# Packed counts and two-part hop tables, with sixteen batches of destinations done densely, in a graph kernel of three passes

## The chip, the cores and the metric

The kernel runs on one NeuronCore of a Trainium2 chip. The metric is the device time of one execution, in microseconds. Five engines matter: PE multiplies matrices, DVE and ACT do elementwise work, POOL issues the gathers of rows, and SP issues nearly all other transfers. Each engine runs its own list of instructions in order, and semaphores tie the lists together.

## What is computed

12,500 nodes with 128 features each, and 212,500 edges sorted by destination (self loops included). Two graph layers follow each other, each behind a layer norm, a ReLU and with a residual:

```python
def reference(x, src, dst, edge_type_2, W_data, b_data, W_control, b_control, W_self, b_self):
    h = relu(layernorm(x))
    # layer 0: a typed message for each edge, summed by destination
    msg = where(edge_type == 0, h[src] @ W_data.T + b_data, h[src] @ W_control.T + b_control)
    x = x + relu(segment_sum(msg, dst) + h @ W_self.T + b_self)
    # layer 1: two hops with symmetric degree norm
    h = relu(layernorm(x)); y = out = h
    for _ in range(2):
        y = segment_sum(y[src] * norm[:, None], dst)
        out = out + y
    return x + out / 3
```

(Names are shortened; `norm` is the product of the inverse square roots of both ends' degrees.)

## The kernel before

The nodes lie in 98 blocks of 128, four blocks to a batch (25 batches, the last with two blocks). The edges lie in 208 groups of 1024, eight chunks of 128 to a group; the last group has five chunks.

After a preparation (messages for each node and type to `typed_table`, indices, bases of the groups) three passes run, k = 0, 1, 2. Each is a loop over slots, and each engine has the same loop with its own part of a slot.

A group, in any pass: POOL issues one indirect DMA for each chunk (`gather`, L874), which brings 128 rows of 512 bytes from the pass's table into a place of `rows` (a ring of `RING` = 4 groups). DVE makes masks that tell to which node of a 128-node window each edge goes (`make_hot`, L1465, in `hot`, a ring of 3, made two groups ahead). PE multiplies mask by rows, eight fp32 matmuls (`sum_rows`, L1091). DVE adds the result to `sums` (`add_group`, L1487). When a batch has all its groups, `cut` closes it, and three slots later `finish` turns it into the next pass's rows: DVE scales (L1395 to L1404), SP stores `scaled` to `hop_table` (`store_nodes`, L732) and the rest to `resid`.

Pass 0 walks all 208 groups. The destinations of the first 15 batches (`DENSE_BATCHES`) are also prepared for the hops: a count of edges from each source node to each destination of a tile of 128 (60 tiles). DVE makes four cells at a time (`make_quad`, a quad; L1509 and L1512 compare cell numbers with `count_up` in PSUM), PE multiplies them (`make_cells`, L1135), ACT turns the 98 x 4 counts of a cell into bytes (`keep_cell`, L1002), and SP stores each tile's strip in DRAM. Between these PE runs matmuls that nothing reads (`fill`, L1126), sixteen per slot in all. The first hop's operand stays in SBUF: `table_parts` holds each scaled block as a high part, rounded to fp32r, and the rest (ACT L982, DVE L1413).

The hops (k = 1, 2) do the first 15 batches by dense products and only the rest by gathering: 82 groups each. A dense step is 14 blocks of one tile's strip against their blocks of `table_parts`: SP loads 224 KB of byte counts (`load_counts`, L772, a ring of `COUNT_RING` = 7 steps; the load for step n + 7 waits until step n is cast), ACT casts them to fp32r (`cast_counts`, L1011, a ring of 3), PE runs 14 matmuls of 256 columns (`dense_step`, L1175). A tile has 7 steps, a hop 420. 18 (hop 1) and 15 (hop 2) of them are lead steps, run behind the last group of the pass before; the others are spread over `DENSE_SLOTS` = 80 of the 82 slots. In hop 1 the last four tiles are done piece by piece, so that pieces of `table_parts` come free early. `read_tile` (L1542) takes a finished tile into `own_in`, and `finish` treats it as a batch.

For hop 2 `table_parts` must hold hop 1's result. SP reloads it from `hop_table` in 14 pieces of 448 KB (`reload`, L783) into a ring of three; ACT copies the high part (`part_high`, L1016), DVE subtracts (`part_low`). These stand in ACT's and DVE's lists ahead of the slot's finish and casts.

What sets the order: in a slot PE sums its group, then runs the slot's dense steps. ACT does reload copies, then the finish, then the slot's casts. DVE adds the group before, makes masks, reads tiles of the slot before, then reload parts and the finish. SP loads counts behind ACT's casts, then reloads, then stores the batch finished one slot before, then loads nodes for a coming one. POOL waits before group o until group o - `RING` is summed, and at the start of a hop until the whole table is stored.

A branch for unevenly spread edges exists on all engines; it isn't taken here.

## Time and profile before

| | us |
|---|---|
| median of 3 runs | 3999.4 (3997.6 to 4004.5) |
| the profiled execution's span | 3997.9 |
| PE busy | 3405.9 (85%) |
| POOL busy | 2879.8 (72%) |
| ACT busy | 2329.7 (58%) |
| DVE busy | 2186.3 (55%) |
| first dense lead step of hop 1 | at 2240.7 |
| slot 0 of hop 1, slot 0 of hop 2 | at 2277.0, at 3158.1 |
| last dense step of hop 2 ends | at 3987.1 |

Busy time is what the profiler saw an engine execute; POOL's issue gaps between gathers aren't in it. The chain of work that ended last goes 38% through POOL's gathers and 34% through the dense matmuls. The three passes have different limits, so a share of the whole span says little; the rows below are from single stretches. A matmul's own duration is longer than its distance to the next, since matmuls overlap; distances between starts are what counts.

### The profile page before, as it was taken

The page shows a single profiled execution, that of the slowest core. Times are in us where ns is not written, and L with a number is a line of the kernel's source. Part 1 is how long each engine was busy: PE and PEld are TensorE (multiplying, and loading weights), DVE is VectorE, ACT ScalarE, POOL GpSimd, SP SyncE. Part 2 cuts the span into 40 slices and gives each one's busy share as a digit, 9 for nine tenths or more (in the row PEclk, how much of TensorE's full clock was granted, in tenths as well). Part 3 has the DMA queues.
Part 4 walks back from the last instruction along what each step waited for, and adds up shares of the span by engine and source line. Part 5 has one row for each costly group of instructions (what it writes and reads, how often), then busy time and mean ns, then how long its engine had stood idle before and what let it go on. Part 6 is the DMA issues. An engine that isn't in the chain of part 4 may idle for free.

```text
span 3997.9 us, 62254 instructions
## 1 busy us (share of the span) xinstructions
PE 3405.9 (85%) x23420; PEld 2729.2 (68%) x23420; DVE 2186.3 (55%) x3333; ACT 2329.7 (58%) x3075; POOL 2879.8 (72%) x3058
## 2 busy tenths in 40 slices
PE   7666777777777787777777899999998899999999
PEld 4344444444444444444444799999998899999999
DVE  7523888888888888888888422222222222222222
ACT  4001444444444444444444688888887788888887
POOL 2677777777777777777777577777776477777775
PEclk9788998999999999999999999999999999999999
DMA  6222333333333334333333566666666666666665
GB/s 194 85 61 61 109 119 121 113 109 110 126 109 110 114 110 128 110 109 125 110 115 112 170 179 187 192 192 187 189 189 184 179 179 176 187 182 181 179 184 145
DMA packets 367268, 571.77 MB, mean 143 GB/s; under 512 B 66678, under 2 KB 308225, under 8 KB 359283
## 3 DMA queue, kind: packets, MB, share of 16 engines
q1 hardware_dynamic: 270435, 370.74, 29.6%
q0 software_dynamic: 95664, 196.60, 19.2%
q8 instruction: 188, 3.08, 0.3%
q14 instruction: 117, 0.96, 0.1%
q10 hardware_dynamic: 864, 0.39, 0.0%
HBM read 424.48 MB, written 142.99 MB: 142 GB/s over the span
## 4 chain that ended last, share of the span: by engine, by line
PE 44%; POOL 38%; issue 13%; DVE 2%; DMA 2%; ACT 1%; SPq 0%; DVEq 0%; POOLq 0%; ACTq 0%
POOL rows L874 38%; PE wide L1175 34%; PE sums_bank L1091 7%; PE wide L1056 1%; ACT strip_ring L1011 1%; DMA stage<-hop_table 1%; DMA rows<-typed_table,index 0%; PE turned_bank L1126 0%; DVE big L1214 0%; DVE rows L1254 0%; DVE stage L1512 0%; POOL stage L914 0%; PE wide L1135 0%; DMA stage<-strips 0%; DMA big<-in_x 0%
## 5 line engine op out<-in xcount | busy, mean ns | idle before, releaser
L874 POOL DMA_INDIRECT rows<-typed_table,index x1661 | 1589.0, 957 | 506.0 <-issue 505.0
L874 POOL DMA_INDIRECT rows<-hop_table,index x1306 | 1251.9, 959 | 481.4 <-issue 394.9
L1011 ACT CAST strip_ring<-stage 128x1792 fp32r<-128x1792 uint8 x840 | 1409.2, 1687 | 285.3 <-PE wide L1175 279.2
L1175 PE MATMUL wide<-table_parts,strip_ring 128*128 128x256 f32 x11760 | 1461.0, 285 | 35.7 <-ACT strip_ring L1011 35.7
L1175 PEld LDWEIGHTS wide<-table_parts,strip_ring 128*128 128x128 f32 x11760 | 1431.3, 193 | 38.0 <-ACT strip_ring L1011 17.5
L1002 ACT CAST stage<-wide 128x392 uint8<-128x392 f32 x1920 | 790.3, 502 | 983.9 <-PE wide L1135 982.6
L1126 PE MATMUL turned_bank<-all_twos 128*128 128x512 bf16 x3328 | 1112.0, 394 | 0.0
L1091 PE MATMUL sums_bank<-rows,hot 128*128 128x129 f32 (+1 forms) x5934 | 801.2, 292 | 287.0 <-DMA rows<-typed_table,index 272.6
L1091 PEld LDWEIGHTS sums_bank<-rows,hot 128*128 128x128 f32 x5934 | 764.4, 206 | 337.8 <-issue 304.0
L1512 DVE TENSOR_TENSOR stage<-count_up,stage 128x1568 bf16<-128x1568 f32 x480 | 855.4, 1782 | 0.0
L1135 PE MATMUL wide<-stage 128*128 128x392 bf16 x1920 | 652.6, 340 | 221.8 <-DVE stage L1512 220.0
L1487 DVE SCALAR_TENSOR_TENSOR sums<-sums_bank,in_upper,sums 128x129 f32 (+1 forms) x372 | 129.8, 349 | 1064.8 <-PE sums_bank L1091 1042.6
L1126 PEld LDWEIGHTS turned_bank<-all_twos 128*128 128x128 bf16 x3328 | 339.0, 102 | 344.6 <-issue 53.5
L1135 PEld LDWEIGHTS wide<-stage 128*128 128x128 bf16 x1920 | 191.9, 100 | 460.2 <-DVE stage L1512 317.5
L1465 DVE TENSOR_TENSOR hot<-count_up,local 128x1024 f32<-128x1024 f32 x372 | 451.8, 1215 | 0.1
L1509 DVE TENSOR_TENSOR stage<-count_up,stage 128x512 bf16<-128x512 f32 x480 | 328.2, 684 | 174.2 <-PE wide L1135 174.0
L1542 DVE TENSOR_REDUCE own_in<-wide 128x128 f32<-128x256 f32 x120 | 50.8, 423 | 356.9 <-PE wide L1175 356.9
L976 ACT ACTIVATE batch_spread<-batch_spread 128x8 f32<-128x8 f32 x25 | 5.4, 216 | 249.6 <-DVE batch_spread L1225 249.6
L1487 DVE SCALAR_TENSOR_TENSOR sums<-sums_bank,base_all,sums 128x129 f32 (+1 forms) x372 | 127.8, 343 | 0.4
L1056 PE MATMUL wide<-stage,rows 128*128 128x384 f32 x196 | 78.5, 528 | 0.0
L1413 DVE TENSOR_TENSOR table_parts<-stage,table_parts 128x896 fp32r<-128x896 f32 x14 | 15.3, 1092 | 73.6 <-ACT table_parts L1016 73.6
L1402 DVE SCALAR_TENSOR_TENSOR xin<-scaled,xin 128x512 f32<-128x512 f32 (+1 forms) x50 | 34.2, 684 | 37.9 <-ACT scaled L945 35.1
(141 smaller groups left out, 669.5 us busy)
## 6 DMA issues: line engine op xcount, KB each, us to landing
stage<-strips SPq DMA_DIRECT2D x840, 224.0 KB
strips<-stage SPq DMA_DIRECT2D x60, 1568.0 KB
rows<-typed_table,index POOLq DMA_INDIRECT x1661
rows<-hop_table,index POOLq DMA_INDIRECT x1306
resid<-xin SPq DMA_DIRECT2D x50, 256.0 KB, 3.0
hop_table<-scaled SPq DMA_DIRECT2D x50, 256.0 KB, 3.8
xin<-resid SPq DMA_DIRECT2D x50, 256.0 KB
typed_table<-rows SPq DMA_DIRECT2D x49, 256.0 KB, 2.1
```

What stands on the lines that cost most here:

```text
L874: pool.indirect_dma_start(out=rows[:, o % RING, c, 0:P], out_offset=None, in_=tables[k], in_offset=bass.IndirectOffsetOnAxis(ap=index[:, c ...
L1002: act.copy(count_strips[tile % 2][:, :, w * CELL:(w + 1) * CELL], wide[:, nth % CELL_BANKS, 0:real_blocks * CELL].rearrange("p (b n) -> p ...
L1011: act.copy(strip_ring[:, number % STRIP_RING], counts_ring[place]).then_inc(strip_cast, 1)
L1056: last = pe.matmul(wide[:, i % 2 * PAIR + b, 0:KINDS * P], normed_t[i % 2][:, b * P:(b + 1) * P], w_all[:, :], start=True, stop=True)
L1091: last = pe.matmul(sums_bank[:, bank, 0:columns], hots[:, c, :], rows[:, slot, c, 0:columns], start=(c == 0), stop=(c == size - 1))
L1126: pe.matmul(turned[:, 0:4 * P].rearrange("p (n f) -> p n f", n=4), all_twos[:, :], all_twos[:, :].unsqueeze(1).to_broadcast([P, 4, P]), st ...
L1135: pe.matmul(wide[:, nth % CELL_BANKS, 0:real_blocks * CELL], quad_low[quad % 2][:, w, :], quad_hot[quad % 2][:, w, :], start=True, stop=Tr ...
L1175: last = pe.matmul(wide[:, nth % 4, 0:PARTS * P], strip_ring[:, number % STRIP_RING, b - first, :], table_parts[:, b, :, :].rearrange("p n ...
L1465: dve.tensor_tensor(hot[:, place, :, :], counting(CHUNKS, P), local[:, group * CHUNKS:(group + 1) * CHUNKS].unsqueeze(2).to_broadcast([P, ...
L1487: last = dve.scalar_tensor_tensor(out=into, in0=sums_bank[:, o % 2, 0:columns], scalar=inside_tile, in1=into, op0=ALU.mult, op1=ALU.add)
L1509: dve.tensor_tensor(quad_low[place], counting(QUAD, P), cell_low[:, cells].unsqueeze(2).to_broadcast([P, QUAD, P]), ALU.is_equal)
L1512: dve.tensor_tensor(quad_hot[place], counting(QUAD, columns), cell_key[:, cells].unsqueeze(2).to_broadcast([P, QUAD, columns]), ALU.is_equ ...
```

## The change

- Hop tables (`hop_table`) hold high part and rest side by side, 1 KB per node where it was 512 bytes. `finish` makes both parts for hop 1's batches too, in `new_parts`, and SP stores them from there, behind `low_ready`.
- Group sums of the hops take fp32r masks and rows of 256 columns; DVE adds both halves, four operations in place of two.
- A reload goes straight into `table_parts`, 896 KB a piece, without work on ACT or DVE; PE waits for its pieces.
- Counts of pass 0: two cells share one matmul result width (2 x 196 columns), since a value carries the count of an even node and, with weight 256, that of the odd one beside it. ACT turns two cells at once into 16-bit words (`keep_pair`). The wide compare has 784 elements in place of 1568, on 16-bit numbers; the narrow compare is four operations with a weight each.
- Sixteen batches are dense: 64 tiles, 448 steps per hop, 73 groups per hop. `DENSE_SLOTS` is 69.
- The rings are smaller: rows 3 groups, masks 2 (made one group ahead), counts 6 steps; three groups are gathered early in place of four.

```diff
-RING = 4
-HOT_RING = 3
-EARLY = 4
+RING = 3
+HOT_RING = 2
+EARLY = 3
...
+CELL_PAIRS = CELLS // 2
+COUNT_BASE = 256
...
-DENSE_BATCHES = 15
+DENSE_BATCHES = 16
...
-COUNT_RING = 7
+COUNT_RING = 6
...
-RELOAD_RING = 3
 RELOADS_AT_ONCE = 3
-STAGE_WORDS = 11264
-DENSE_SLOTS = 80
+STAGE_WORDS = 10112
+DENSE_SLOTS = 69
...
-    tables = [typed_table] + [nc.dram_tensor(f"hop_table{n}", (padded, P), F32, kind="Internal").ap() for n in range(HOPS)]
+    tables = [typed_table] + [nc.dram_tensor(f"hop_table{n}", (real_blocks * P, PARTS * P), F32, kind="Internal").ap() for n in range(HOPS)]
...
+        rows = sbuf("rows", [RING, CHUNKS, PARTS * P], F32R)
+        hot = sbuf("hot", [HOT_RING, CHUNKS, P], F32R)
 
...
-        reloaded = [region(reload_words) for _ in range(RELOAD_RING)]
+        new_parts = [region(NODE_BLOCKS * PARTS * P, F32R).rearrange("p (b n f) -> p b n f", b=NODE_BLOCKS, n=PARTS)
+                     for _ in range(2)]
 
...
+        def parts_of(n, k, s, general):
+            if general or k:
+                return new_parts[n % 2][:, 0:held(s)]
+            return table_parts[:, s * NODE_BLOCKS:s * NODE_BLOCKS + held(s)]
 
...
-            def store_nodes(n, k, s):
+            def store_nodes(n, k, s, general):
                 if k < HOPS:
                     sp.wait_ge(resid_ready, n + 1)
                     sp.dma_start(of_batch(resid, s), in_blocks(xin[:, n % XIN, :])).then_inc(resid_stored[n % XIN], 16)
-                    sp.wait_ge(scaled_ready, n + 1)
-                    sp.dma_start(of_batch(tables[k + 1], s), in_blocks(scaled[:, n % 2, :])).then_inc(table_stored[n % 2], 16)
+                    sp.wait_ge(low_ready, n + 1)
+                    first, end = s * BATCH, s * BATCH + held(s) * P
+                    sp.dma_start(tables[k + 1][first:end, :].rearrange("(b p) f -> p b f", p=P),
+                                 parts_of(n, k, s, general).rearrange("p b n f -> p b (n f)").bitcast(F32)
+                                 ).then_inc(table_stored[n % 2], 16)
                     return
                 first, end = s * NODE_BLOCKS, min((s + 1) * NODE_BLOCKS, whole)
...
-                def reload(r, piece):
+                def reload(piece):
                     for s in reload_batches(piece):
                         n = event_of[1][s]
                         sp.wait_ge(table_stored[n % 2], 16 * count_of(n + 1, 2, n % 2))
                     sp.wait_ge(strip_used, last_step_with(piece) + 1)
-                    if r >= RELOAD_RING:
-                        sp.wait_ge(reload_low, r - RELOAD_RING + 1)
                     first = piece * RELOAD_BLOCKS
-                    sp.dma_start(in_blocks(reloaded[r % RELOAD_RING], RELOAD_BLOCKS),
+                    sp.dma_start(table_parts[:, first:first + RELOAD_BLOCKS].rearrange("p b n f -> p b (n f)").bitcast(F32),
                                  tables[2][first * P:(first + RELOAD_BLOCKS) * P, :].rearrange("(b p) f -> p b f", p=P)
-                                 ).then_inc(reload_in[r % RELOAD_RING], 16)
+                                 ).then_inc(reload_in[piece], 16)
...
                     pool.indirect_dma_start(
-                        out=rows[:, o % RING, c, 0:P], out_offset=None, in_=tables[k],
+                        out=rows[:, o % RING, c, 0:width_of(k)].bitcast(F32), out_offset=None, in_=tables[k],
...
-            def finish(n, k, s, splits):
+            def finish(n, k, s, general):
...
-                if splits:
-                    first, blocks = s * NODE_BLOCKS, held(s)
+                if k < HOPS:
                     act.wait_ge(scaled_ready, n + 1)
-                    act.copy(table_parts[:, first:first + blocks, 0, :], in_blocks(scaled[:, n % 2, 0:blocks * P], blocks)).then_inc(high_ready, 1)
+                    act.copy(parts_of(n, k, s, general)[:, :, 0, :], in_blocks(scaled[:, n % 2, 0:held(s) * P], held(s))
+                             ).then_inc(high_ready, 1)
...
-                def part_high(r, piece):
-                    first = piece * RELOAD_BLOCKS
-                    act.wait_ge(reload_in[r % RELOAD_RING], 16 * (r // RELOAD_RING + 1))
-                    act.copy(table_parts[:, first:first + RELOAD_BLOCKS, 0, :], in_blocks(reloaded[r % RELOAD_RING], RELOAD_BLOCKS)
-                             ).then_inc(reload_high, 1)
-
...
-                                    keep_cell(quad * QUAD + w)
-                        if k == 1:
-                            for r, piece in reloads_of_slot(i - 1):
-                                part_high(r, piece)
+                                for w in range(QUAD // 2):
+                                    keep_pair(quad * QUAD // 2 + w)
                         finishing = event_at(k, i - 3)
-                        if finishing and k == 0:
-                            finish(finishing[0], k, finishing[1], True)
+                        if finishing and k < HOPS:
+                            finish(finishing[0], k, finishing[1], False)
...
-            def sum_rows(bank, slot, size, hots, columns):
+            def sum_rows(k, bank, slot, size, hots):
                 for c in range(size):
-                    last = pe.matmul(sums_bank[:, bank, 0:columns], hots[:, c, :], rows[:, slot, c, 0:columns],
-                                     start=(c == 0), stop=(c == size - 1))
+                    ends = dict(start=(c == 0), stop=(c == size - 1))
+                    if k == 0:
+                        last = pe.matmul(sums_bank[:, bank, 0:TILE], hots[:, c, :].bitcast(F32), rows[:, slot, c, 0:TILE].bitcast(F32), **ends)
+                    else:
+                        last = pe.matmul(sums_bank[:, bank, 0:PARTS * P], hots[:, c, :], rows[:, slot, c, :], **ends)
                 return last
...
                     elif tile < LEAD_TILES:
-                        pe.wait_ge(reload_low, reloads_before(first, end))
+                        for piece_in in range(first // RELOAD_BLOCKS, (end - 1) // RELOAD_BLOCKS + 1):
+                            pe.wait_ge(reload_in[piece_in], 16)
...
                                          op0=ALU.mult, op1=ALU.add).then_inc(resid_ready, 1)
                 dve.tensor_tensor(in_blocks(values, blocks), in_blocks(values, blocks), over_features(factors, blocks), ALU.mult
                                   ).then_inc(scaled_ready, 1)
-                if splits:
-                    dve.wait_ge(scaled_ready, n + 1)
-                    part_low(s * NODE_BLOCKS, blocks, in_blocks(values, blocks), high_ready, n + 1, low_ready)
-
-            def part_low(first, blocks, values, parted, count, ready):
-
-                dve.wait_ge(parted, count)
-                dve.tensor_tensor(table_parts[:, first:first + blocks, 1, :], values,
-                                  table_parts[:, first:first + blocks, 0, :].bitcast(F32), ALU.subtract).then_inc(ready, 1)
+                dve.wait_ge(scaled_ready, n + 1)
+                dve.wait_ge(high_ready, n + 1)
+                parts = parts_of(n, k, s, general)
+                dve.tensor_tensor(parts[:, :, 1, :], in_blocks(values, blocks), parts[:, :, 0, :].bitcast(F32), ALU.subtract
+                                  ).then_inc(low_ready, 1)
...
-                        last = dve.scalar_tensor_tensor(out=into, in0=sums_bank[:, o % 2, 0:columns], scalar=inside_tile, in1=into,
-                                                        op0=ALU.mult, op1=ALU.add)
-                    last.then_inc(added, 1)
+
+                    def add_columns(start):
+                        for n, inside_tile in enumerate((in_upper[:, group:group + 1], in_lower[:, group:group + 1])):
+                            into = flat_sums[:, ds(base - tile_place(first) + n * TILE, columns)]
+                            last = dve.scalar_tensor_tensor(out=into, in0=sums_bank[:, o % 2, start:start + columns], scalar=inside_tile,
+                                                            in1=into, op0=ALU.mult, op1=ALU.add)
+                        return last
+
+                    if k:
+                        add_columns(0).then_inc(half_added, 1)
+                        dve.wait_ge(half_added, o - groups + 1)
+                        add_columns(P).then_inc(added, 1)
+                    else:
+                        add_columns(0).then_inc(added, 1)
...
-                    columns = real_blocks * CELL
-                    dve.tensor_tensor(quad_hot[place], counting(QUAD, columns),
-                                      cell_key[:, cells].unsqueeze(2).to_broadcast([P, QUAD, columns]), ALU.is_equal
+                        dve.wait_ge(strip_made, (quad - 1) * QUAD // 2)
+                    first = quad * QUAD % (CELL_BATCHES * P)
+                    for w in range(QUAD):
+                        cell = slice(first + w, first + w + 1)
+                        dve.tensor_scalar(quad_low[place][:, w, :], count_up, cell_low[:, cell], cell_weight[:, cell],
+                                          ALU.is_equal, ALU.mult)
+                    dve.tensor_tensor(quad_hot[place], count_quads,
+                                      cell_key[:, first:first + QUAD].unsqueeze(1).to_broadcast([P, hot_columns, QUAD]), ALU.is_equal
                                       ).then_inc(strip_hot_ready, 1)
...
-                        if i < slots_of(k) and o + 2 < n_places:
-                            make_hot(o + 2)
+                        if i < slots_of(k) and o + 1 < n_places:
+                            make_hot(o + 1)
...
-                        if k == 1:
-                            for r, piece in reloads_of_slot(i - 1):
-                                part_low(piece * RELOAD_BLOCKS, RELOAD_BLOCKS, in_blocks(reloaded[r % RELOAD_RING], RELOAD_BLOCKS),
-                                         reload_high, r + 1, reload_low)
```

## Rows read from the trace of the kernel before

**Rows 1.** Stretches: us, busy PE, PEld, DVE, ACT, POOL (instructions), PE clock, DMA share, GB/s

```profile
1000.00:1100.00 100.00, 76.86 (x435) 45.29 (x434) 85.36 (x114) 46.95 (x114) 75.92 (x80) 0.93 0.40 126
...
2500.00:2600.00 100.00, 100.00 (x848) 100.00 (x847) 26.29 (x49) 82.30 (x50) 75.66 (x80) 1.00 0.68 190
```

**Rows 2.** Page, group of POOL's gathers in pass 1: count, busy, mean ns, idle before

```profile
L874 POOL DMA_INDIRECT rows<-typed_table,index x1661 | 1589.0, 957 | 506.0 <-issue 505.0
```

**Rows 3.** PE in order of time: start, us, instructions; then page, dense matmuls

```profile
2277.01 1.95 PE L1091 MATMUL sums_bank<-rows,hot 128*128 128x128 f32 x16
...
2288.87 1.95 PE L1091 MATMUL sums_bank<-rows,hot 128*128 128x128 f32 x16
...
2299.04 1.94 PE L1091 MATMUL sums_bank<-rows,hot 128*128 128x128 f32 x16
...
L1175 PE MATMUL wide<-table_parts,strip_ring 128*128 128x256 f32 x11760 | 1461.0, 285 | 35.7 <-ACT strip_ring L1011 35.7
```

**Rows 4.** POOL and PE in order of time: a gather, then the sum of its group

```profile
129.06 1.65 POOL L874 DMA_INDIRECT rows<-typed_table,index  x1 [0.30 <-issue]
...
143.04 3.81 PE L1091 MATMUL sums_bank<-rows,hot 128*128 128x129 f32 x16 [14.12 <-DVE hot L1465]
...
1910.35 0.94 POOL L874 DMA_INDIRECT rows<-typed_table,index  x1 [0.30 <-issue]
...
1925.32 1.95 PE L1091 MATMUL sums_bank<-rows,hot 128*128 128x129 f32 x16
...
2254.71 0.94 POOL L874 DMA_INDIRECT rows<-hop_table,index  x1 [23.06 <-DMA hop_table<-scaled]
```

**Rows 5.** PE in order of time, end of hop 1 and start of hop 2

```profile
3061.28 11.13 PE L1175 MATMUL wide<-table_parts,strip_ring 128*128 128x256 f32 x70 [5.79 <-ACT strip_ring L1011]
...
3117.66 3.06 PE L1091 MATMUL sums_bank<-rows,hot 128*128 128x128 f32 x26
...
3158.06 1.95 PE L1091 MATMUL sums_bank<-rows,hot 128*128 128x128 f32 x16
```

**Rows 6.** Groups of instructions by line and form: ACT's copies of reloaded tables

```profile
L1016 ACT CAST table_parts<-stage 128x896 fp32r<-128x896 f32 x14 | 13.1, 937 | 35.7 <-DMA stage<-hop_table 35.7
```

**Rows 7.** PE in order of time, the last sums of hop 2

```profile
3987.10 3.06 PE L1091 MATMUL sums_bank<-rows,hot 128*128 128x128 f32 x26
```

**Rows 8.** Groups by line and form, DVE and ACT: busy us, mean ns of one

```profile
L1011 ACT CAST strip_ring<-stage 128x1792 fp32r<-128x1792 uint8 x840 | 1409.2, 1687 | 285.3 <-PE wide L1175 279.2 <-DMA stage<-strips 6.1
...
L1512 DVE TENSOR_TENSOR stage<-count_up,stage 128x1568 bf16<-128x1568 f32 x480 | 855.4, 1782 | 0.0
...
L1509 DVE TENSOR_TENSOR stage<-count_up,stage 128x512 bf16<-128x512 f32 x480 | 328.2, 684 | 174.2 <-PE wide L1135 174.0
...
L1542 DVE TENSOR_REDUCE own_in<-wide 128x128 f32<-128x256 f32 x120 | 50.8, 423 | 356.9 <-PE wide L1175 356.9
...
L1413 DVE TENSOR_TENSOR table_parts<-stage,table_parts 128x896 fp32r<-128x896 f32 x14 | 15.3, 1092 | 73.6 <-ACT table_parts L1016 73.6
...
L982 ACT CAST table_parts<-scaled 128x512 fp32r<-128x512 f32 x24 | 14.8, 617 | 32.7 <-DVE scaled L1404 32.7
...
L1395 DVE TENSOR_TENSOR scaled<-own_in,inv 128x512 f32<-128x512 f32 x15 | 10.2, 679 | 0.0
...
L1530 DVE SCALAR_TENSOR_TENSOR stage<-wide,cell_line 128x128 f32<-128x128 f32 x15 | 4.2, 283 | 2.8 <-PE wide L1153 2.8
```

**Rows 9.** DMA queues in 2500 to 2600, then 250 to 350: packets, MB, share

```profile
q1 hardware_dynamic: 11808, 13.60, 46.1%
q0 software_dynamic: 2553, 5.22, 20.9%
...
stage<-strips SPq DMA_DIRECT2D x49, 224.0 KB
...
q1 hardware_dynamic: 3168, 1.57, 5.5%
```

**Rows 10.** GB/s of all transfers in 2.5 us slices from 1000 us

```profile
GB/s 347 321 135 52 59 52 52 52 52 52 133 401 266 52 52 56 52 52 52 214 127 52 59 52 52 52 52 267 321 288 85 54 52 52 52 52 114 396 284 67
```

More of the change, by code:

```diff
@@ L608, in reloads_of_slot @@
         def reloads_of_slot(i):
-            return [(r, piece) for r, (slot, piece) in enumerate(reload_order) if slot == i]
-        def reloads_before(first, end):
-            return max(r for r, (_, piece) in enumerate(reload_order)
-                       if piece * RELOAD_BLOCKS < end and (piece + 1) * RELOAD_BLOCKS > first) + 1
+            return [piece for slot, piece in reload_order if slot == i]
         assert all(lead_steps[k] <= LEAD_AT_ONCE * LAST for k in range(1, HOPS + 1))
@@ L1353, in take_degrees, with finish @@
                 dve.tensor_scalar(spread_now[:, 1, :], degree, 1.0, None, ALU.max).then_inc(degree_read, 1)
-            def finish(n, k, s, source, read, splits, own=None):
+            def finish(n, k, s, source, read, general, own=None):
                 blocks = held(s)
```

115 lines of the change are left out of this document (67 added, 48 removed).

## The prediction

> **What bounds the kernel now.** I read the stretches first, then for each stretch the engine that never pauses, then the seams between stretches.
>
> Pass 1 runs to about 2235 us. In a 100 us stretch of it POOL is busy 75.9 us, and the rest is the 0.30 us gap behind each of its 80 gathers [rows 1, 2]: one gather costs 1.25 us, a group of eight 10.0 us, and in 1661 gathers POOL waits 1 us in all for anything but its own issuing [rows 2]. PE (77 us of 100) and DVE (85) have room. Pass 1 is POOL's.
>
> In the hops PE is busy 100 us of 100, and POOL still issues 80 gathers per 100 us [rows 1]. A slot is one group summed and five dense steps: 2288.87 to 2299.04, 10.17 us. Slot 0 has six steps and lasts 11.86 us [rows 3], so a step (14 matmuls of 256 columns) costs 1.69 us, 0.121 us a matmul, and the eight fp32 matmuls of a group 1.72 us. POOL begins hop 1 at 2254.71 [rows 4], 22 us ahead of slot 0, and keeps that lead. So PE sets the hops, with POOL 2% behind it: cheaper matmuls alone would soon meet POOL, and only fewer gathers let both fall.
>
> The ideal length of hop 1's dense slots is 402 x 1.69 + 80 x 1.72 = 817 us (420 steps less 18 lead steps). The rows show 2277.01 to 3117.66, 840.7 us [rows 3, 5]: 24 us are stalls, all at the end, where PE waits for strips, as 5.79 us at 3061.28 [rows 5]. ACT is late because its list there holds copies of reloaded tables: it waits 35.7 us for their transfers [rows 6] and casts nothing meanwhile. From 3117.66 to slot 0 of hop 2 at 3158.06 are 40.4 us [rows 5]; from there to 3987.10, 829 us; from there to the end 10.8 [rows 7].
>
> **The change, part by part.** *Pass 1.* The sixteenth batch adds one gather of cells, 1.25 us on POOL: +1.3 us. The count work (512 quads for 480) isn't on POOL. A quad costs DVE 1.78 + 0.68 us now [rows 8]. Its new wide compare has 784 elements, half of 1568: 0.9 us if it goes by elements, up to the 1.09 us of the 896-element subtraction; the four low compares are 0.15 us each (128 of 512 elements) to 0.28 (the 128-element op from PSUM) [rows 8]. That is 1.5 to 2.2 us a quad, 4.2 to 6.2 us per slot against 6.5 now, so the cover stays and I take nothing. If DVE exceeded 10 us a slot, the excess would count in full.
>
> The ring of rows falls from four groups to three. The latest sum of pass 1 began 15 us after POOL issued its group's last gather (1910.35 to 1925.32, largest of 207 pairs) [rows 4]; with its 1.95 us that is 17, and POOL needs the place 20 us after that issue began. So no wait. At the start the first sum comes 14 us after its group and takes 3.8 us: 18 against 20.
>
> *Gathers.* Hop groups fall from 82 to 73, each gather brings 1 KB rows, and sums become 256-column fp32r matmuls. That is the dense form, so I take 0.121 us, 0.97 us a group. The dearest it could be is today's 1.72 us. POOL's cost goes by rows, 128 as before: 10.0 us a group against a slot that becomes longer, so POOL drops off the path.
>
> *Dense work.* 448 steps a hop, 430 in slots in hop 1 and 433 in hop 2 (18 and 15 lead steps), over 69 slots: 430 x 1.69 + 69 x 0.97 = 793.6 us and 433 x 1.69 + 67 = 798.7 us. A slot is 11.5 us. ACT casts 1.68 us a step [rows 8], 10.5 us a slot: it keeps only 1 us of slack where it had 1.8.
>
> *ACT's new place in hop 1.* The split of a finished batch into high and rest parts moves from the reload to the finish. So ACT waits, once per batch, for DVE's scaled values, copies them in 0.62 us, and the next slot's casts are queued behind. DVE in turn first reads tiles of the slot before. From a tile's last matmul: read 0.42, three steps of the finish near 0.7 each with their waits, 2.5 us; then copy 0.62 and cast 1.68 [rows 8]. PE meanwhile has the d steps behind that tile and one group sum. The stall is 2.6 + 0.62 + 1.68 + 0.3 - 0.97 - 1.69 d, or 4.2 - 1.7 d. The planner's formulas give d = 1 for two batches, d = 2 for eight, and three or more (or no tile) for the rest: 2 x 2.5 + 8 x 0.9 = 12 us. Between the ends 0 (ACT ahead through other slack) and 24 x 4.2 = 101 I take 12.
>
> *Transfers.* In the hop stretch the row queue takes 20.9% of 16 engines for 80 gathers, 4.2 us a gather. The other queue takes 46.1% for 49 strips and nine batch transfers; these cost 14.7 us each (six in 5.5%), so a strip costs 12.4 [rows 9]. After: strips 6.2 x 12.4 = 77, batch traffic 20, gathers 8 x 4.2 to 8 x 8.4 (by row, or by byte) = 34 to 67. That is 131 to 164 us of 184 per slot, 71 to 89%; now it is 68%. I take the upper part of it. Strips are asked for six steps ahead, now seven. A batch's three transfers then hold the queue 3.5 us; I put 3 us of stalls on hop 2.
>
> *Reloads.* ACT's and DVE's splits go, and with them the 24 us. But each piece is now 896 KB, near 50 us of engine time, and eight of them are asked for between slots 64 and 68, on the same queue as the strips. In these 45 us: 24 strips 300, gathers 270, reloads 400, others 50, together 1020 us against 720. That is 19 us too much; prefetched strips and rows absorb a part. I take 12 us, with 0 and 20 as ends. The Trainium skill's page "DMA: Bandwidth & Descriptors", section Specifications, gives one core near 358 GB/s of HBM. By that the 18 MB of this stretch need 51 us, 6 more than it has. The trace has slices of 396 and 401 GB/s [rows 10], above that limit, though those are stores of counts.
>
> *Seam.* Slots 69 to 72 hold sums alone. With three places POOL can't issue group 72 before group 69 is summed, so its five gathers (6.3 us) and the landing put that sum 10 us past the dense end, where it was done after 3. Now ACT casts no lead strip before batch 23 is split: DVE adds (four operations a group now), makes masks and finishes batches 15 and 23, which brings ACT to about 15 us; the first lead step starts near 17, and 15 lead steps take 25.4. The seam is 42.4 us. Batch 24 is stored by then (25 us) and POOL's first group landed (37 us). Late reloads have the 25 us too. At the end of hop 2: sum at 10, adds, clearing, finish, store: 16.5 us where it is 10.8.
>
> **Sum.** 2277.0 + 1.3 = 2278.3. Hop 1: 793.6 + 12 + 12 = 817.6 -> 3095.9. Seam 42.4 -> 3138.3. Hop 2: 798.7 + 3 -> 3940.0. End 16.5 -> 3956.5, against a span of 3997.9: 41 us less. The median lies 1.5 us above the span, so 3958. Of the 41 us, 23 come from each hop's ideal, 19 from stalls replaced by smaller ones; the ends give 8 back.
>
> **Rivals.** *Nothing collides (3931).* The 12, 12 and 3 us don't appear. For it: in the whole trace PE waits for strips only 35.7 us, all near seams [rows 3]. Against: ACT's slack halves. 0.18.
>
> *Transfers pace the hops (3986).* Late strips cost 0.2 us per slot, 138 slots, 28 us. For it: 89% is an average, and batch traffic comes in bursts. Against: today's strips are never late inside a hop. To lose the whole gain a slot must reach 11.8 us, which needs 189 us of transfers, or 11.5 us a gather against at most 8.4. 0.17.
>
> *ACT is held at each finish (slower, up to 4046).* If DVE answers so late that each of 24 finishes costs the full 4.2 us, 88 us come on top. It decides at 2.2 us each: 12 + 41 = 53 over 24. For it: ACT, DVE and PE then wait in a ring. Against: DVE is busy 26 us of 100 in the hops [rows 1]. 0.07.
>
> *The change doesn't do what it says (4068).* If fp32r masks and rows cost what fp32 costs now, each of 146 groups is 0.75 us dearer, +110 us. Against: the dense rows have the very form. 0.04.
>
> *A port lock in pass 1.* DVE's new count operations read and write 16-bit values; were each of the 2048 small compares to hold POOL's descriptor writes for its 0.15 us, pass 1 would grow by 300 us. For it nothing: in the midst of pass 1 POOL's gathers keep 0.94 us [rows 4]. The Trainium skill's page "SBUF — State Buffer", section Who interferes with whom, has VectorE lock GpSimd out in its two-port modes; the counting operand stays in PSUM here, which the skill excludes from them. 0.02.
>
> **Chances.** Forecast 0.52; 3931: 0.18; 3986: 0.17, of which 0.05 lie within no change; the three slower ones 0.13, of which 0.01 does, as a mild form. A measurement of this kernel tells 0.2% (8 us) from no change. Faster 0.82, same 0.06, slower 0.12. The range takes in 3931, below it 10 us for the seam and masks, and 3986, above it the rest of the transfer bounds: 3920 to 4000.
>
> **What would show it.** Hop slots of 11.5 us with PE full; group sums at 0.97 us; POOL waiting for PE in each hop slot; pass 1 unchanged and gathers at 1.25 us; in hop 1 short PE waits for strips behind finishes, none in hop 2; the last sum some 10 us behind the last dense step; no copies of reloaded tables on ACT. Wrong would be: transfers near 100%, slots above 11.8 us, a gather above 1.3 us, or POOL waiting for sums in pass 1.

## The result

| | median, us | lowest to highest | ratio to before (95% interval) |
|---|---|---|---|
| before | 3998.5 | 3997.6 to 4004.5 | |
| after | 3954.5 | 3953.1 to 3955.9 | 0.9889 (0.9877 to 0.9901) |
| after, once more, beside the experiments | 3951.1 | 3948.8 to 3957.6 | 0.9887 (0.9870 to 0.9903) |

The change takes 44 us off: 3954.5, where 3958 was forecast. The profiled execution of the kernel after has a span of 3952.7 us (3956.5 was summed). In its time line the places of the sum can be read one by one (us):

| | before | forecast | after |
|---|---|---|---|
| slot 0 of hop 1 begins | 2277.0 | 2278.3 | 2281.6 |
| dense slots of hop 1 last | 840.7 | 817.6 | 810.0 |
| from there to slot 0 of hop 2 | 40.4 | 42.4 | 49.7 |
| dense slots of hop 2 last | 829.0 | 801.7 | 794.2 |
| from there to the end | 10.8 | 16.5 | 17.2 |

Stretches of the kernel after, one in pass 1 and one in hop 1 (columns as in [rows 1]):

```profile
1000.00:1100.00 100.00, 80.97 (x427) 49.91 (x425) 65.91 (x199) 29.55 (x62) 75.62 (x81) 0.90 0.36 111
2500.00:2600.00 100.00, 99.01 (x825) 98.60 (x824) 29.50 (x60) 90.93 (x58) 65.97 (x69) 1.00 0.81 243
```

In pass 1 POOL's 75.6 us are what they were [rows 1], though DVE fell from 85 to 66 us and ACT from 47 to 30. In the hop PE is still full, POOL fell from 75.7 to 66.0 us and now has slack, ACT rose to 91 and the transfers from 68% to 81%.

Groups of the page after, in the columns of [rows 2] and [rows 3] (the gathers of pass 1, ACT's casts, the dense matmuls, the gathers of the hops, the group sums of the hops):

```profile
L890 POOL DMA_INDIRECT rows<-typed_table,index x1661 | 1589.9, 957 | 506.1 <-issue 505.9
L1027 ACT CAST strip_ring<-stage 128x1792 fp32r<-128x1792 uint8 x896 | 1494.4, 1688 | 137.8 <-PE wide L1188 115.5
L1188 PE MATMUL wide<-table_parts,strip_ring 128*128 128x256 f32 x12544 | 1539.0, 284 | 28.6 <-ACT strip_ring L1027 26.0
...
L890 POOL DMA_INDIRECT rows<-hop_table,index x1162 | 1109.7, 955 | 599.7 <-issue 314.2
...
L1102 PE MATMUL sums_bank<-rows,hot 128*128 128x256 f32 x1162 | 163.6, 284 | 15.8 <-DMA rows<-hop_table,index 10.6
```

A gather of 1 KB rows costs POOL 955 ns, one of 512 byte rows 957: its cost goes by rows, as taken. Beyond that, POOL waits in the hops 240 us for group sums, where it waited 3 us for them before:

```profile
POOL rows L890 <- PE sums_bank L1102: 239.9, 135, 7.4
```

(From the waits of POOL between 2280 and 3950: us in all, times, longest.) PE in order of time shows an undisturbed slot, group sum and six steps:

```profile
2294.23 1.11 PE L1102 MATMUL sums_bank<-rows,hot 128*128 128x256 f32 x8
2295.18 10.22 PE L1188 MATMUL wide<-table_parts,strip_ring 128*128 128x256 f32 x84
2305.24 1.11 PE L1102 MATMUL sums_bank<-rows,hot 128*128 128x256 f32 x8
```

From start to start the sum takes 0.95 us, the six steps 10.06, the slot 11.01. A slot of seven steps takes 12.68. Of 69 slots 16 have seven: 16 x 12.68 + 53 x 11.01 = 786.4 us is the ideal of hop 1, and 23.6 of its 810.0 us are stalls.

### The profile page after: what moved, and what is told of

Its sections match the earlier page's. It is cut to its first block, busy times and chain, and to the rows that moved or that the text cites. A ratio compares the mean times of both kernels' runs of the same rounds, so it can differ in the third digit from the quotient of the medians.

```text
span 3952.7 us, 62194 instructions
## 1 busy us (share of the span) xinstructions
PE 3401.3 (86%) x22892; PEld 2748.3 (70%) x22892; DVE 1925.3 (49%) x5238; ACT 2121.5 (54%) x2246; POOL 2739.2 (69%) x2915
## 4 chain that ended last, share of the span: by engine, by line
PE 41%; POOL 40%; issue 13%; DVE 2%; DMA 2%; ACT 1%; SPq 0%; POOLq 0%; DVEq 0%; ACTq 0%
POOL rows L890 40%; PE wide L1188 36%; PE sums_bank L1102 3%; ACT strip_ring L1027 1%; PE wide L1063 1%; DMA stage<-strips 1%; POOL stage L930 0%; DVE big L1232 0%; DVE flat L1272 0%; DMA hop_table<-stage 0%; DVE xin L1420 0%; DVE scaled L1413 0%; DMA big<-in_x 0%; DVE scaled L1422 0%; PE turned_bank L1136 0%
## 5 line engine op out<-in xcount | busy, mean ns | idle before, releaser
L1188 PEld LDWEIGHTS wide<-table_parts,strip_ring 128*128 128x128 f32 x12544 | 1524.5, 193 | 32.2 <-ACT strip_ring L1027 17.1
L890 POOL DMA_INDIRECT rows<-hop_table,index x1162 | 1109.7, 955 | 599.7 <-issue 314.2
L1018 ACT CAST stage<-wide 128x392 uint16<-128x392 f32 x1024 | 497.0, 485 | 1277.9 <-PE wide L1145 1271.6
L1100 PE MATMUL sums_bank<-rows,hot 128*128 128x129 f32 x3322 | 514.9, 319 | 362.5 <-DMA rows<-typed_table,index 346.1
L1538 DVE TENSOR_SCALAR stage<-counts,stage 128x128 bf16<-128x128 int16 x2048 | 559.6, 335 | 470.2 <-PE wide L1145 469.9
L1145 PE MATMUL wide<-stage 128*128 128x196 bf16 x2048 | 687.5, 336 | 99.1 <-DVE stage L1540 99.1
L1507 DVE SCALAR_TENSOR_TENSOR sums<-sums_bank,in_upper,sums 128x128 f32 (+1 forms) x500 | 174.7, 349 | 915.4 <-PE sums_bank L1102 676.3
L1483 DVE TENSOR_TENSOR hot<-counts,local 128x1024 fp32r<-128x1024 int16 x354 | 429.5, 1213 | 0.1
L1540 DVE TENSOR_TENSOR stage<-counts,stage 128x784 bf16<-128x784 int16 x512 | 283.7, 554 | 0.0
L1102 PE MATMUL sums_bank<-rows,hot 128*128 128x256 f32 x1162 | 163.6, 284 | 15.8 <-DMA rows<-hop_table,index 10.6
L1507 DVE SCALAR_TENSOR_TENSOR sums<-sums_bank,base_all,sums 128x128 f32 (+1 forms) x500 | 171.2, 342 | 0.7
```

The lines of the kernel that those rows point to most:

```text
L890: pool.indirect_dma_start(out=rows[:, o % RING, c, 0:width_of(k)].bitcast(F32), out_offset=None, in_=tables[k], in_offset=bass.IndirectOff ...
L1018: act.copy(paired_strips[tile % 2][:, :, w * CELL:(w + 1) * CELL].rearrange("p b (c n) -> p b c n", c=2), wide[:, nth % CELL_BANKS, 0:2 * ...
L1100: last = pe.matmul(sums_bank[:, bank, 0:TILE], hots[:, c, :].bitcast(F32), rows[:, slot, c, 0:TILE].bitcast(F32), **ends)
L1102: last = pe.matmul(sums_bank[:, bank, 0:PARTS * P], hots[:, c, :], rows[:, slot, c, :], **ends)
L1145: made = pe.matmul(wide[:, nth % CELL_BANKS, half * hot_columns:(half + 1) * hot_columns], quad_low[quad % 2][:, w, :], quad_hot[quad % 2] ...
L1188: last = pe.matmul(wide[:, nth % 4, 0:PARTS * P], strip_ring[:, number % STRIP_RING, b - first, :], table_parts[:, b, :, :].rearrange("p n ...
```

## The experiments

The kernel after ran again in the first set, to tell its own spread from the rest:

> The changed kernel again, as the reference of this set: 3954 us.

Ratios are to the kernel before, run on the same chip beside them (its median is 3998.9 beside a1 and e1 to e3, 4000.1 beside e4 to e9).

| kernel | median, us | ratio (95% interval) |
|---|---|---|
| e1: before, sixteen batches in 69 slots | 4064.1 | 1.0160 (1.0143 to 1.0177) |
| e2: after, fifteen batches in 78 slots | 3942.3 | 0.9862 (0.9846 to 0.9879) |
| e3: before, counts packed | 4000.8 | 1.0006 (0.9997 to 1.0016) |
| e4: after, three casts ahead of the finish | 3941.4 | 0.9854 (0.9838 to 0.9870) |
| e5: after, half of each reload | 3940.3 | 0.9848 (0.9832 to 0.9865) |
| e7: e4 with 71 slots | 3934.6 | 0.9837 (0.9820 to 0.9853) |
| e9: e2 with e4's order | 3938.1 | 0.9845 (0.9828 to 0.9861) |

### e1. The sixteenth batch alone

```
-DENSE_BATCHES = 15
+DENSE_BATCHES = 16
...
-DENSE_SLOTS = 80
+DENSE_SLOTS = 69
```

> The kernel before with sixteen dense batches, dense steps over 69 slots, and nothing else of the change (fp32 sums, 512-byte rows, unpacked counts). Theory (PE sets the hops): a slot is 6.2 steps of 1.68 us and a sum of 1.79 us, 12.2 us; the dense slots of a hop take 843 and 848 us where they ideally take 817 and 822, the reload stalls of 24 us and the seams stay, pass 1 gets 1.3 us longer. Together about 4055 us, 55 slower than before. Rival (fewer gathers are what saves): 72 gathers less in each hop at 1.25 us, 90 us a hop, about 3820 us. A second rival: DVE's 512 unpacked quads (2.46 us each, 90% of a slot in pass 1) begin to delay sums, and pass 1 ends more than 5 us later as well.

It costs 65 us. PE in order of time, at the end of hop 1:

```profile
3061.94 11.99 PE L1175 MATMUL wide<-table_parts,strip_ring 128*128 128x256 f32 x98
...
3082.23 12.17 PE L1175 MATMUL wide<-table_parts,strip_ring 128*128 128x256 f32 x84 [6.51 <-ACT strip_ring L1011]
...
3118.88 12.57 PE L1175 MATMUL wide<-table_parts,strip_ring 128*128 128x256 f32 x84 [5.12 <-ACT strip_ring L1011]
```

An added batch is 28 steps, 47 us of PE in each hop, for nine groups dropped, 16 us of PE with fp32 sums. PE set the hops already, so the time rises: the dense slots of the two hops last 28 and 27 us longer (869.0 and 855.9), the seam 7 and the end 3, with four sums behind the last dense slot and not two. Pass 1 isn't later (slot 0 of hop 1 at 2276.4), though DVE was busy 90 us of 100 in it.

### e2. All the rest without it

```
-DENSE_BATCHES = 16
+DENSE_BATCHES = 15
...
-DENSE_SLOTS = 69
+DENSE_SLOTS = 78
```

> The changed kernel with fifteen dense batches again (82 groups a hop, dense steps over 78 slots); two-part tables, fp32r sums, direct reloads and packed counts stay. Theory: a slot needs 9.6 us of PE and 10.0 us of POOL, so POOL sets the hops: 653 gathers take 816 us from POOL's start near 2256 to 3074, about 18 us from the last sum to its restart, 816 us again and some 12 us to the end: about 3920 us, and PE waits for rows in most slots. Rival (the sixteenth batch carries the gain): about 3998 us, as before. Third: 1 KB rows at POOL's full pace need 89% of the transfer engines; if they can't keep up, slots pass 10.4 us and the time 3950 us.

It is faster than the kernel after, by 9 to 12 us. The stretch 2500 to 2600 and, in order of time, PE and then POOL:

```profile
2500.00:2600.00 100.00, 100.00 (x838) 100.00 (x838) 36.06 (x73) 91.15 (x59) 75.93 (x80) 1.00 0.84 258
```

```profile
2505.34 1.11 PE L1102 MATMUL sums_bank<-rows,hot 128*128 128x256 f32 x8
2506.29 8.54 PE L1188 MATMUL wide<-table_parts,strip_ring 128*128 128x256 f32 x70
2514.66 1.11 PE L1102 MATMUL sums_bank<-rows,hot 128*128 128x256 f32 x8
...
3083.05 2.04 PE L1102 MATMUL sums_bank<-rows,hot 128*128 128x256 f32 x8 [8.59 <-DMA rows<-hop_table,index]
3090.01 1.41 PE L1102 MATMUL sums_bank<-rows,hot 128*128 128x256 f32 x5 [4.91 <-DMA rows<-hop_table,index]
```

```profile
3083.87 0.95 POOL L890 DMA_INDIRECT rows<-hop_table,index  x1 [0.30 <-issue]
3105.10 0.94 POOL L890 DMA_INDIRECT rows<-hop_table,index  x1 [20.28 <-DMA hop_table<-stage]
```

A five-step slot needs 9.32 us of PE against 10.0 of POOL. POOL now runs from 2256.7 to 3083.9 with 0.9 us of waits for sums, and the last sums wait for its rows. So POOL sets the length of the hops, as the theory said. But PE doesn't wait for rows in most slots, though that was expected: in the stretch shown PE is full, since it had lost time to ACT in three slots (as behind 2492.1, 13.24 us) and works that off; from 2707 on it catches up with POOL again and again. It waits for rows 30 times in the two hops, 56 us in all, 35 of them behind the last dense slots. The price of a hop is what POOL costs: 82 groups in 828 us and 20.3 us until the next table is stored, 848 in all from POOL's start in hop 1 to its start in hop 2. The kernel after needs 810.0 + 49.7 = 859.7 from slot 0 to slot 0. The expected 3920 was too low by 19 us. Nearly all of it is the gathers: 653 of them were put at 816 us a hop and took 828 and 824, since some last 1.1 to 1.5 us and not 0.95. From slot 0 of hop 1 (2281.4) to slot 0 of hop 2 (3123.8) e2 takes 842.4 us, 17.3 less than the kernel after, and from there to the end (3938.8) 815.0, 3.6 more. How the gain over the kernel before divides between fp32r sums and direct reloads was not tried.

### e3. The packed counts alone

The wide compare and the low compares, ACT's copy of pairs and PE's pairs, put into the kernel before:

```
...
-                    dve.tensor_tensor(quad_low[place], counting(QUAD, P), ...)
...
+                    for w in range(QUAD):
...
+                        dve.tensor_scalar(quad_low[place][:, w, :], count_up, cell_low[:, cell], cell_weight[:, cell], ...)
...
```

> The kernel before with the packed counts alone (two cells in one result, 784-element compare, half of ACT's copies); all else as before. Theory: pass 1 is set by POOL's gathers, and the count work lies beside them: the end of pass 1 within 1 us, the time within 3 us of 3998. Rival (the count work is on the path of pass 1): DVE falls by 10 to 20 points of the stretch, and pass 1 is shorter by tens of us. Third: 16-bit operations of DVE lock POOL out, gathers above 1.25 us and pass 1 longer.

No change: the interval reaches from 0.9997 to 1.0016. The stretch 1000 to 2200 of the kernel before and of this one:

```profile
1000.00:2200.00 1200.00, 920.92 (x5105) 551.24 (x5105) 1017.39 (x1355) 548.04 (x1332) 909.26 (x955) 0.92 0.37 115
```

```profile
1000.00:2200.00 1200.00, 952.38 (x5109) 601.63 (x5110) 777.47 (x2317) 337.64 (x708) 909.29 (x955) 0.89 0.37 115
```

240 us of DVE and 210 of ACT are gone from this stretch, and POOL's busy time is the same to 0.03 us. Work was taken from engines that had cover. Slot 0 of hop 1 begins at 2273.8, 3.2 us earlier than before, where 1 us was expected at most; but the kernel after differs by 5 us from run to run in this place (2281.6 and 2276.2), and the medians show no gain.

### e4. ACT's finish behind three casts

```
+                        now = steps_at(k, i)
+                        ahead = min(3, len(now)) if k == 1 and i <= 64 else 0
+                        for number in now[:ahead]:
+                            cast_counts(number)
                         ...finish...
-                        for number in steps_at(k, i):
+                        for number in now[ahead:]:
                             cast_counts(number)
```

> The changed kernel, but in the dense slots of hop 1 up to slot 64 ACT does the first three casts of a slot ahead of the finish's copy, and only then waits for DVE's scaled values. Theory (ACT's wait inside its list makes the ten short PE waits of hop 1, 10.9 us in slot lengths): all ten vanish, every slot of hop 1 up to 64 is 11.01 or 12.68 us, and the time falls by 11 us, to about 3942. Rival (the strips come late because transfers are at 81%): the waits stay where they are, since the order on ACT moves no transfer, time 3953. Third: DVE, now held longer by ACT at each finish, delays masks or adds, and new waits on DVE appear in PE's sums: slower.

Ten slots of the kernel after are longer than 11.01 or 12.68 us before slot 64, one of them this (ACT, then PE, in order of time):

```profile
2446.48 0.62 ACT L997 CAST stage<-scaled 128x512 fp32r<-128x512 f32 x1 [3.28 <-DVE scaled L1422]
```

```profile
2445.50 1.11 PE L1102 MATMUL sums_bank<-rows,hot 128*128 128x256 f32 x8
2448.74 11.84 PE L1188 MATMUL wide<-table_parts,strip_ring 128*128 128x256 f32 x84 [2.13 <-ACT strip_ring L1027]
2460.42 1.11 PE L1102 MATMUL sums_bank<-rows,hot 128*128 128x256 f32 x8
```

With the casts first, the same stretch of this kernel's PE:

```profile
2448.09 1.11 PE L1106 MATMUL sums_bank<-rows,hot 128*128 128x256 f32 x8
2449.05 10.22 PE L1192 MATMUL wide<-table_parts,strip_ring 128*128 128x256 f32 x84
2459.10 1.11 PE L1106 MATMUL sums_bank<-rows,hot 128*128 128x256 f32 x8
```

All ten are gone: every slot to 3029.59 takes 11.01 or 12.69 us, and the dense slots of hop 1 last 797.2 us in place of 810.0. So the waits were ACT's order, and nothing else took their place. The slots of the reloads are as long as before (11.9, 16.4 and 15.6 us).

### e5. Half of each reload

The rest parts keep their old values, so hop 2 computes with them; all the rest is done.

```
-  sp.dma_start(table_parts[:, first:first + RELOAD_BLOCKS].rearrange(...).bitcast(F32),
-               tables[2][first * P:(first + RELOAD_BLOCKS) * P, :]...
+  sp.dma_start(table_parts[:, first:first + RELOAD_BLOCKS, 0, :].bitcast(F32),
+               tables[2][first * P:(first + RELOAD_BLOCKS) * P, 0:P]...
```

> The changed kernel with each reload cut to the high parts (448 KB for 896); the rest parts in table_parts keep hop 1's old values, so hop 2's dense products are computed from wrong rest parts. Theory (the reloads on the strips' queue delay the strips at the end of hop 1): the stalls of slots 64 to 68 (11 us) fall to 4 us or less, and the 2.7 us wait for a strip inside the lead steps shrinks as well; together 8 to 11 us less, about 3944. Rival (SP's wait for the last use of a piece, which holds back the next strip loads, is the cause, not the bytes): the stalls stay above 8 us and the time within 3 us of 3953.

PE in order of time, first of the kernel after, then of this one:

```profile
3047.23 1.11 PE L1102 MATMUL sums_bank<-rows,hot 128*128 128x256 f32 x8
...
3064.03 12.97 PE L1188 MATMUL wide<-table_parts,strip_ring 128*128 128x256 f32 x84 [3.18 <-ACT strip_ring L1027]
...
3091.54 2.07 PE L1102 MATMUL sums_bank<-rows,hot 128*128 128x256 f32 x16
```

```profile
3057.99 1.11 PE L1102 MATMUL sums_bank<-rows,hot 128*128 128x256 f32 x8
3058.94 10.22 PE L1188 MATMUL wide<-table_parts,strip_ring 128*128 128x256 f32 x84
3068.99 1.11 PE L1102 MATMUL sums_bank<-rows,hot 128*128 128x256 f32 x8
```

The three reload slots of the kernel after take 12.5, 17.1 and 14.7 us; here they take 11.01, 11.00 and 11.45. The order of SP's list and the number of transfers are the same, so the cause is the bytes. The 2.7 us wait inside the lead steps was expected to shrink with them and did not (2.78 us at 3112.13): it has another cause, shown below where the seam is explained. The queues of the kernel after from 3045 to 3092 (packets, MB, share of 16 engines) show the load:

```profile
DMA packets 12675, 16.31 MB, mean 347 GB/s; under 512 B 1012, under 2 KB 11735, under 8 KB 12673
...
q1 hardware_dynamic: 11255, 12.43, 80.5%
q0 software_dynamic: 1418, 3.84, 23.7%
```

The shares add to 104%, so the packets of this stretch took more engine time than it has, and ACT waits up to 4.4 us for its strips.

### e7. e4 with 71 slots

```
-DENSE_SLOTS = 69
+DENSE_SLOTS = 71
```

> The kernel of casts first (above), with the dense steps over 71 slots in place of 69. Theory (behind the last dense step the last group's sum waits 12 us since its rows can't be asked for before group 69 is summed): with two dense slots more the rows are there, the last sum ends 3 us behind the last dense step; the two slots add 2 us a hop, the end of hop 2 shrinks from 17 us to about 11, net 4 to 5 us less there and 0 to 5 less at the seam: 3932 to 3938. Rival (the finish of the last batches, not the sum, ends the hop): the end stays at 17 us and the time at that of casts first or 2 to 4 us above.

This asks what the sums cost that stand alone behind the dense slots. PE at both ends of a hop:

```profile
3076.70 1.71 PE L1106 MATMUL sums_bank<-rows,hot 128*128 128x256 f32 x13
3091.96 12.26 PE L1192 MATMUL wide<-table_parts,strip_ring 128*128 128x256 f32 x84 [13.54 <-ACT strip_ring L1027]
...
3919.52 1.71 PE L1106 MATMUL sums_bank<-rows,hot 128*128 128x256 f32 x13
```

The last two groups now come together, 1.7 us long. At the end of hop 2 that pays: 11.6 us to the end (3931.1) against 17.2 (17.4 in e4). At the seam it pays little: 46.7 us against 48.9 in e4, no more than the 49.7 and 47.0 of the two profiled runs of the kernel after differ by. The last sums aren't late there any more (+12.8 us in the kernel after), but the first lead step begins at +15.3 where it began at +17.8 in the kernel after, behind the finishes of batches 15 and 23. This is the fastest kernel, 17 to 20 us below the two medians of the kernel after.

### e9. e2 with e4's order

The same edit of ACT's loop, up to slot 72, in the kernel with fifteen batches.

> Fifteen dense batches with all the rest of the change, dense steps over 78 slots (3942 us before), and casts first on ACT up to slot 72 of hop 1. Theory (there POOL sets the hops and PE waits for rows): the short waits behind finishes vanish from PE's slots, but the time stays within 3 us of 3942, since POOL's last gather of a hop doesn't move. Rival (PE still sets hop 1 with fifteen batches): 8 to 11 us less, about 3932.

It gives 4 us, a little more than the 3 expected, where e4 gave 10 to 13. The dense slots of hop 1 last 790.3 us where they lasted 791.0 in e2: where POOL sets the pace, a stall on PE is absorbed. Of the two best versions the one with sixteen batches is 3.5 us faster, with ranges that don't meet (3932.8 to 3937.1, 3937.6 to 3940.0). But with the order on ACT alone (e4, 3941.4) it is not, and other numbers of slots were not tried with fifteen.

## Why the prediction held, and where it was off

*What bounds.* PE in the hops, POOL in pass 1: right for both kernels. e1 shows the first (28 steps more and eleven sums less in the dense slots are 47 - 19.5 = 27.5 us of PE, and the dense slots grew by 28 and 27 us), e3 the second.

*"Only fewer gathers let both fall."* This was wrong. e2 gathers as often as the kernel before and is 57 us faster. I had compared slots, 10.17 us of PE with 10.0 of POOL. But POOL's own path from hop to hop is 848 us (e2), where PE's was 840.7 + 40.4 = 881: its lead of 22 us and PE's 24 us of stalls were room as well. fp32r sums and direct reloads together use it; a five-step slot fell from 10.17 to 9.32 us, 0.85 a group. With them in place the sixteenth batch costs 17 us up to slot 0 of hop 2 and brings 4 behind it, a loss of 9 to 12 us by the medians. I had not asked what each part gives with the others in place, and so gave the batch credit for the whole. Only with ACT's order and the slots mended was sixteen the better number (e7), against fifteen with the order alone (e9).

*Pass 1.* No effect of the counts, as put. The wide compare was put at 0.9 to 1.1 us and takes 0.55; the low ones take 0.335 each by the record (0.15 to 0.28 was put); 1.9 us a quad, within the 1.5 to 2.2:

```profile
L1538 DVE TENSOR_SCALAR stage<-counts,stage 128x128 bf16<-128x128 int16 x2048 | 559.6, 335 | 470.2 <-PE wide L1145 469.9
...
L1540 DVE TENSOR_TENSOR stage<-counts,stage 128x784 bf16<-128x784 int16 x512 | 283.7, 554 | 0.0
```

Nothing hung on it. Slot 0 came 3.3 us later than forecast in this run, 2.1 us earlier in the second run of the same kernel (2276.2). In both PE waits 5 to 6 us for casts among the lead steps; they began 5 us later here (2243.1 against 2237.8). What moves the end of pass 1 by that much was not tried.

*The split of the sum.* The prediction says of its 41 us that 23 come from each hop's ideal, 19 from smaller stalls, and that the ends give 8 back. That doesn't add up, and its own terms say otherwise: 23 + 23 from the ideals, nothing from the stalls of hop 1 (24 for 24), 4 from those of hop 2 (7 for 3), and 9 back at the start, the seam and the end.

*The hops' ideal.* 793.6 was put and 786.4 measured. Both its terms were too large. Over all undisturbed slots one more step costs 1.68 us in both kernels (before, five and six steps: 10.17 and 11.855 in the mean; after, six and seven: 11.007 and 12.687), where I had 1.69 from two rounded slots: 430 x 0.01 = 4.3 us. The rest of a slot is the group, 11.007 - 6 x 1.68 = 0.93, where 0.97 was put: 3 us over 69 slots. The same working gives the old group 1.77 us and not 1.72: five steps last 8.47 us to the next sum behind an fp32 sum (before, 2290.57 to 2299.04) and 8.37 behind an fp32r one (e2, 2506.29 to 2514.66). So the slots got 7 us shorter a hop than put, twice.

*Stalls by finishes.* 12 us was put, ten slots, two of them large. Ten came: two of 2.4 and 3.9 us, eight of 0.73 to 0.81, 12.4 in all (10.9 in the second run). The formula 4.2 - 1.7 d gave their number and nearly their sizes; e4 shows the cause. The one of 3.9 us is 2.4 in the second run, behind the same wait:

```profile
2443.44 10.34 PE L1188 MATMUL wide<-table_parts,strip_ring 128*128 128x256 f32 x84 [2.13 <-ACT strip_ring L1027]
```

There the granted clock was 1.00 during these 84 matmuls; in the first run (11.84 us, shown under e4) it was 0.85 in the mean.

*Reloads.* 12 put, 11.3 measured (1.5 + 6.1 + 3.7); e5 shows the cause. But only some 7 us of them are waits: the matmuls behind the waits last 12.97 and 11.83 us for 10.22, at a mean granted clock of 0.77 and 0.85. The prediction had no such term, and its 12 fits so well in part by luck. Of 810.0 us all is accounted for: 786.4 + 12.4 + 11.3.

The rule of the Trainium skill that I weighed for the reloads (page "DMA: Bandwidth & Descriptors", section Specifications, near 358 GB/s of HBM for one core) fits in the mean, 347 GB/s over 47 us, and not as a ceiling: slices of 1.2 us within it reach 398 and 402. The Trainium skill's page "HBM Reference", section Specifications (TRN2), says that a core that streams alone measures well above the share and is bounded by its 16 DMA engines. The 104% agree with that.

*Hop 2.* 3 us of stalls were put and 2.8 measured, but that is luck. They were put for strips that come late behind a batch's transfers, and no such slot came; the 2.8 us are all in slot 0 (15.49 for 12.68), and 5.7 in the second run (18.34). The kernel before has 6.8 us there (18.62 for 11.86), which the prediction doesn't use. In the kernel after the profile names nobody that PE waits for in this slot, so the cause stays open.

*Transfers.* Put in the upper part of 71 to 89%; 81% came. The row queue takes 32.8% for 69 gathers in the stretch, 7.6 us a gather against 4.2 [rows 9]: by bytes, not by rows. Outside the reload slots and the seams no slot was lengthened by a strip (each has its ideal length or a finish in it).

*The seam.* 42.4 put, 49.7 measured: a miss of 7.3 us (4.6 in the second run, 47.0; seam and slot 0 behind it together take 65.2 and 65.3). The first lead step at +17.8 (put 17) and the last sum at +12.8 (put 10) were near. The 15 lead steps were put at 25.4 and take 31.9:

```profile
3109.36 12.54 PE L1188 MATMUL wide<-table_parts,strip_ring 128*128 128x256 f32 x84 [3.58 <-ACT strip_ring L1027]
3124.60 16.83 PE L1188 MATMUL wide<-table_parts,strip_ring 128*128 128x256 f32 x126 [2.70 <-ACT strip_ring L1027]
3141.27 1.11 PE L1102 MATMUL sums_bank<-rows,hot 128*128 128x256 f32 x8
```

```profile
3092.00:3109.00 17.00, 4.23 (x27) 3.56 (x25) 13.49 (x28) 2.61 (x3) 5.48 (x5) 0.66 0.87 286
3109.00:3122.00 13.00, 12.54 (x84) 12.37 (x84) 4.22 (x9) 8.74 (x7) 0.00 (x0) 0.79 0.84 258
3122.00:3141.00 19.00, 16.40 (x124) 16.43 (x125) 0.00 (x0) 17.78 (x11) 14.19 (x15) 0.91 0.86 262
3142.00:3160.00 18.00, 15.42 (x130) 15.25 (x129) 5.29 (x14) 13.37 (x9) 13.44 (x15) 1.00 0.88 278
```

(The stretches in the columns of [rows 1].) 2.7 us are a wait for ACT, which waits 3.8 us for strips there. ACT and then SP in order of time:

```profile
3118.55 0.40 ACT L997 CAST stage<-scaled 128x256 fp32r<-128x256 f32 x1
3122.77 4.86 ACT L1027 CAST strip_ring<-stage 128x1792 fp32r<-128x1792 uint8 x3 [3.82 <-DMA stage<-strips]
```

```profile
3119.50 0.36 SPq L748 DMA_DIRECT2D hop_table<-stage  x1
3119.91 18.62 SPq L790 DMA_DIRECT2D stage<-strips  x15
```

ACT has cast the six strips of the ring by then. SP asks for more only behind the store of batch 24, and that store waits for ACT's copy, which stands behind the six casts. In e5, with half the bytes, it is the same (store at 3106.96, strips from 3107.36), and so is PE's wait. The kernel before has the like: its next strips are asked for at 3136.93, behind its last store, and PE waits 2.35 us there. The other 4 us are matmuls that last longer: PE was busy 4 us of the 17 before, and the mean granted clock was 0.79 and then 0.91 in these stretches, before it was 1.00 again. I priced lead steps at the rate of a full hop. The trace of the kernel before shows better at its own seam, where 98 matmuls, 11.9 us in a full hop, follow a pause:

```profile
3127.79 13.74 PE L1175 MATMUL wide<-table_parts,strip_ring 128*128 128x256 f32 x98 [7.07 <-ACT strip_ring L1011]
```

Its 15 lead steps take 30.3 us (to 3158.06), 5 more than I put. Whether another price would return with an earlier start of the lead steps was not tried: e7 starts them 2.5 us earlier after its last dense step and its first block still takes 12.3 us.

*The end.* 16.5 put, 17.2 measured. e7 shows that 5.6 us of it are the two sums that stand alone, which the prediction put down to the ring of three; no run changes the ring by itself. e1, with a ring of four and as many sums alone, ends in 13.9 us. At the seam the lone sums cost 2 us at most (46.7 against 48.9), since ACT's finishes stand behind them: there the step of the prediction that named ACT as last was right.

So the terms off were -7.6 and -7.5 (hops), +7.3 (seam), +3.3 (start) and +0.7 (end): -4 together. The forecast is closer than its parts, and that is luck: 15 us too much in the hops and 11 too little outside them.

*The rivals.* None came: not all stalls vanished, no slot reached 11.8 us through transfers, finishes cost 0.5 us each in the mean over 24 and not 4.2, sums have the dense price, and gathers beside 16-bit compares keep 957 ns in pass 1, so no port lock shows.

## What to carry to other kernels

When a change has several parts that feed one another, ask for each what it gives with all others in place, with the engine that is second in mind: here cheaper sums and plain reloads gave 57 us together, and more dense work, which looked like their condition, cost some 10 until the order on ACT and the number of slots were right. Put work that waits for another engine behind the work that somebody is waiting for, where the list allows it. Price the first matmuls after a pause from rows behind a pause.

## What was not expected of the hardware

- A gather of 128 rows takes POOL 0.955 us whether a row has 512 bytes or 1 KB; the transfer takes 4.2 and 7.6 us of engine time. So longer rows are free on POOL and not on the queues.
- DVE's compare of 784 16-bit elements with an operand in PSUM took 554 ns, 0.71 ns an element, where the fp32 one of 1568 took 1782, 1.14 ns an element [rows 8]. The 1024-element fp32r mask made from 16-bit counts takes 1213 ns, 1.18 an element: the gain came where input and output both had 16 bits.
- A short pause of PE can cost more than its length. Behind the 3.18 us wait at 3064.03 the granted clock was 0.50 from 3065 to 3070, the lower of its two levels (1.2 GHz for 2.4), and PE had 26 matmuls in these 5 us, where it had 44 from 3071 to 3076 at 1.00. Behind a wait of 2.13 us it came out both ways, 0.85 in one run and 1.00 in the other, in the same slot of the same kernel.
- PE in pass 1 got a lower mean granted clock where the count matmuls have 196 columns and not 392: from 1000 to 2200 it was 0.90 after and 0.89 in e3, 0.92 before and 0.94 in e1. (A value between is a mean over the two levels.) The time of pass 1 didn't follow, since POOL sets it.
